# Rel products split by bank for both axes, and evacuated by one instruction per engine

## The reference

```python
attn = einsum('bqd,bkd->bqk', q * scale, k)
rel_h = einsum('bhwc,hkc->bhwk', q, Rh)      # Rh[h, k] = rel_pos_h[h - k + 13]
rel_w = einsum('bhwc,wkc->bhwk', q, Rw)      # Rw[w, k] = rel_pos_w[w - k + 13]
attn = attn + rel_h[..., :, None] + rel_w[..., None, :]
out = softmax(attn) @ v
x = x + out @ proj_w + proj_b
```

## Time and profile before

| | |
|---|---|
| median of 3 runs | 2332.41 us (2329.14 to 2334.24) |
| the profiled execution | 2339.97 us, its span 2338.2 us |
| TensorE busy | 2094.7 us, 90% of the span, 27904 matmuls |
| VectorE busy | 1653.4 us, 71% |
| ScalarE busy | 1621.4 us, 69% |
| GpSimd busy | 714.4 us, 31% |
| DMA | 216.34 MB, mean 93 GB/s |
| mean granted clock of TensorE | 0.978 |

### The profile page before, as it was taken

How to read it: one execution, slowest core, us unless ns; L and a number is a source line. 1 busy time by engine, 2 the same in 40 slices (tenths; PEclk the granted TensorE clock), 3 DMA queues, 4 the chain that set the end, 5 groups by cost and what they waited for, 6 DMA issues and landing times.

```text
span 2338.2 us, 73485 instructions
## 1 busy us (share of the span) xinstructions
PE 2094.7 (90%) x27904; PEld 1595.9 (68%) x27904; DVE 1653.4 (71%) x3923; ACT 1621.4 (69%) x3713; POOL 714.4 (31%) x1796
## 2 busy tenths in 40 slices
PE   1899999999999989999999999899989999999998
PEld 1677676776767767667667766677766766777765
DVE  5677777667767677777677777677767777777675
ACT  0577777677767667767676777677767776777675
POOL 1233323333333233333233333233223333333230
PEclk9899999999999999999999999999999999999999
DMA  1333434333434333433333443344334343334331
GB/s 47 84 94 95 104 91 105 91 92 91 103 93 97 90 94 93 101 93 93 91 98 91 94 103 96 88 96 100 91 91 102 94 100 93 94 93 103 91 92 47
DMA packets 170550, 216.34 MB, mean 93 GB/s; under 512 B 29783, under 2 KB 138072, under 8 KB 170202
## 3 DMA queue, kind: packets, MB, share of 16 engines
q1 hardware_dynamic: 170202, 211.64, 37.7%
HBM read 117.00 MB, written 57.80 MB: 75 GB/s over the span
## 4 chain that ended last, share of the span: by engine, by line
PE 39%; DMA 33%; SPq 14%; DVE 6%; issue 4%; ACT 3%; POOL 1%; POOLq 0%; ACTq 0%; DVEq 0%
PE ps_m L412 18%; DMA q_st<-mrow 17%; DMA k_dram<-qk_hl 10%; PE ps_sc L538 7%; PE ps_max L525 6%; SPq L375 6%; DMA q_dram<-qk_hl 6%; DVE qk_hl L734 4%; PE ps_o L557 3%; SPq L382 3%; ACT qk_hl L598 2%; SPq L341 2%; SPq L387 2%; PE ps_m L501 2%; DVE rel_hl L776 1%
## 5 line engine op out<-in xcount | busy, mean ns | idle before, releaser
L722 DVE TENSOR_REDUCE mx<-ps_max 98x2 f32<-98x392 f32 x1536 | 819.4, 562 | 232.6 <-PE ps_max L525 215.5
L586 ACT ACTIVATE probs<-ps_sc 98x392 f32<-98x392 f32 x1536 | 714.5, 497 | 232.3 <-PE ps_sc L538 198.2
L525 PE MATMUL ps_max<-k_st,q_st 124*98 124x196 f16 x3072 | 548.9, 261 | 82.4 <-DVE mx L722 82.1
L538 PE MATMUL ps_sc<-q_st,k_st 125*98 125x196 f16 x3072 | 523.3, 252 | 95.6 <-DMA q_st<-mrow 94.1
L776 DVE TENSOR_TENSOR rel_hl<-ps_m,rel_hi 64x504 f16<-64x504 f32 (+1 forms) x768 | 431.4, 562 | 162.0 <-ACT rel_hi L643 152.9
L525 PEld LDWEIGHTS ps_max<-k_st,q_st 124*98 124x98 f16 x3072 | 295.0, 126 | 296.4 <-issue 198.0
L538 PEld LDWEIGHTS ps_sc<-q_st,k_st 125*98 125x98 f16 x3072 | 320.9, 126 | 123.1 <-DMA q_st<-mrow 120.4
L557 PE MATMUL ps_o<-probs,v_st 98*32 98x196 f32 x6144 | 389.6, 340 | 0.5 <-ACT o_sb L578 0.5
L634 ACT ACTIVATE rel_hi<-ps_m,is_lo 64x504 f16<-64x504 f32 (+1 forms) x384 | 223.9, 583 | 189.1 <-PE ps_m L471 185.7
L471 PE MATMUL ps_m<-q_st,rel_st 64*32 64x84 f16 x7168 | 341.6, 266 | 4.8 <-DVE rel_hl L776 4.5
L809 POOL TENSOR_TENSOR msq<-mv 96x2 f32<-96x2 f32 x128 | 24.4, 191 | 1007.1 <-DVE mv L748 1007.1
(11 more groups left out here) (72 smaller groups left out, 3293.8 us busy)
## 6 DMA issues: line engine op xcount, KB each, us to landing
q_st<-q_dram SPq DMA_DIRECT2D x128, 294.0 KB, 3.8
k_st<-k_dram SPq DMA_DIRECT2D x256, 147.0 KB, 3.9
q_dram<-qk_hl SPq DMA_DIRECT2D x128, 147.0 KB, 2.6
k_dram<-qk_hl SPq DMA_DIRECT2D x128, 147.0 KB, 2.7
q_st<-rel_hl SPq DMA_DIRECT2D x256, 73.5 KB
q_st<-rel_hl SPq DMA_DIRECT2D x256, 64.3 KB
xa<-in_x SPq DMA_DIRECT2D x64, 147.0 KB
xd<-in_x SPq DMA_DIRECT2D x64, 147.0 KB
```

The lines of the kernel that those rows point to most:

```text
L525: last = nc.tensor.matmul(ps_max[head % 2][0:HT, h * TOK:h * TOK + TOK], q_st[u.r][0:R_MAX, head, h, :], k_st[u.r][0:R_MAX, head, :], star ...
L538: last = nc.tensor.matmul(ps_sc[head % 2][0:HT, kt * TOK:kt * TOK + TOK], k_st[u.r][0:STACK, head, kt * HT:kt * HT + HT], q_st[u.r][0:STAC ...
L586: nc.scalar.activation(probs[head][:, :, :], ps_sc[head % 2][0:HT, 0:2 * TOK].rearrange("p (k t) -> p k t", k=2), ACT.Exp, scale=1.0 / (QS ...
L722: nc.vector.reduce_max(mx[u.r % 2][:, head, :], ps_max[head % 2][0:HT, 0:2 * TOK].rearrange("p (q k) -> p q k", q=2), axis=AX.X).then_inc( ...
```

## The change

Before, the column products of an image column with index a were computed for all 14 image rows at once, 84 columns in a matmul (6 heads x 14), and bank n held the image columns of its share. After, bank n holds the tokens of its own image rows for both axes: for each bank there are 14 column products in each half, with 6 heads x 6, 6 or 2 tokens. The row products are the same. Both axes then have the same layout in a bank, so one ScalarE instruction and one VectorE instruction over 128 partitions evacuate it. The DMAs, the banks and the order of the jobs stay.

```diff
-        def rel_views(dst, ps, n, a0):
-            by_row = (dst[0:64, :, a0 * SIDE:(a0 + n) * SIDE],
-                      ps[0:64, 0:n * HH * SIDE].rearrange("p (h x) -> p h x", h=HH))
-            by_col = (dst[64:128, :, :].rearrange("p h (a b) -> p (h a) b", a=SIDE)[:, :, a0:a0 + n],
-                      ps[64:128, 0:n * HH * SIDE].rearrange("p (x b) -> p x b", b=n))
-            return by_row, by_col
+        def rel_part(dst, n):
+            a0 = sum(RELB[:n])
+            return dst[:, :, a0 * SIDE:(a0 + RELB[n]) * SIDE]
+
+        def rel_bank(n):
+            return ps_m[BANK[f"rel{n}"]][:, 0:RELB[n] * HH * SIDE].rearrange("p (h x) -> p h x", h=HH)
...
-                    for i in range(rows):
-                        a = sum(RELB[:n]) + i
-                        for axis in range(2):
-                            w = 2 * (SIDE - 1 - a)
+                    a0 = sum(RELB[:n])
+                    for i in range(SIDE):
+                        for axis in range(2) if i < rows else (1,):
+                            w = 2 * (SIDE - 1 - (i if axis else a0 + i))
                             for half in range(2):
+                                p = 64 * axis + 32 * half
+                                to = ps[p:p + RW, 0:rows * HH * SIDE].rearrange("p (h t) -> p h t", h=HH)\
+                                    .rearrange("p h (a b) -> p h a b", b=SIDE)
                                 q = q_st[u.r][0:R_REL, half * HH:half * HH + HH, :, :]\
-                                    .rearrange("p h q t -> p h (q t)")
-                                p = 64 * axis + 32 * half
-                                to = ps[p:p + RW, 0:rows * HH * SIDE]
+                                    .rearrange("p h q t -> p h (q t)")[:, :, a0 * SIDE:(a0 + rows) * SIDE]\
+                                    .rearrange("p h (a b) -> p h a b", b=SIDE)
                                 if axis == 0:
-                                    to = to.rearrange("p (h a b) -> p h a b", h=HH, a=rows)[:, :, i, :]
+                                    to, q = (part[:, :, i, :] for part in (to, q))
                                 else:
-                                    to = to.rearrange("p (x b) -> p x b", b=rows)[:, :, i]
-                                last = nc.tensor.matmul(
-                                    to, rel_st[:, lay, axis, w:w + RW],
-                                    q[:, :, a * SIDE:a * SIDE + SIDE] if axis == 0 else q[:, :, a::SIDE],
-                                    start=True, stop=True)
+                                    to, q = (part[:, :, :, i] for part in (to, q))
+                                last = nc.tensor.matmul(to, rel_st[:, lay, axis, w:w + RW], q, start=True, stop=True)
...
-                            dst, src = rel_views(rel_hi[u.r % 2], ps_m[BANK[f"rel{n}"]], RELB[n], sum(RELB[:n]))[0]
-                            nc.scalar.activation(dst, src, ACT.Identity, scale=is_lo[0:64, 0:1])
...
-                            dst, src = rel_views(rel_hi[u.r % 2], ps_m[BANK[f"rel{n}"]], RELB[n], sum(RELB[:n]))[1]
-                            nc.scalar.activation(dst, src, ACT.Identity, scale=is_lo[64:128, 0:1])\
-                              .then_inc(s_rhi, 1)
+                            nc.scalar.activation(rel_part(rel_hi[u.r % 2], n), rel_bank(n), ACT.Identity,
+                                                 scale=is_lo[:, 0:1]).then_inc(s_rhi, 1)
...
-                            for (h, src), (l, _) in zip(hi, lo):
-                                last = nc.vector.tensor_tensor(l, src, h, ALU.subtract)
-                            last.then_inc(s_rlo, 1)
+                            nc.vector.tensor_tensor(rel_part(rel_hl[u.r % 2], n), rel_bank(n),
+                                                    rel_part(rel_hi[u.r % 2], n), ALU.subtract).then_inc(s_rlo, 1)
```

More of the change, by code:

```diff
@@ L771, in iteration @@
                                 wait_dma(dve, s_rel, b4, 4)
-                            hi, lo = (rel_views(part[u.r % 2], ps_m[BANK[f"rel{n}"]], RELB[n], sum(RELB[:n]))
-                                      for part in (rel_hi, rel_hl))
                             dve.wait_ge(s_rhi, u.n * 3 + n + 1)
-                            for (h, src), (l, _) in zip(hi, lo):
-                                last = nc.vector.tensor_tensor(l, src, h, ALU.subtract)
-                            last.then_inc(s_rlo, 1)
+                            nc.vector.tensor_tensor(rel_part(rel_hl[u.r % 2], n), rel_bank(n),
+                                                    rel_part(rel_hi[u.r % 2], n), ALU.subtract).then_inc(s_rlo, 1)
                     u = due(unit, s, AT["oT"] + DVE_LATER["oT"])
```

## The result

The changed kernel takes 2436.03 us (median of 4 runs, 2419.9 to 2441.05), the kernel before on the same chip 2330.77. The ratio is 1.044 (95% interval 1.039 to 1.050): slower by 4.4%, where 2.0% was forecast. The profiled execution spans 2437.4 us against 2338.2, 99 more.

A forecast was written before the change was run, and what follows sets the result against it. The prediction took the round of transfers to pace the units at 17.6 us. Evacuations, TensorE growth and the first wait counted 0, lower clock +48 us; with the 2332.4 us median this gave 2380 us, range 2308 to 2420.

The forecast's parts named there:

- What bounds the kernel: Whole unit: the round of transfers through SyncE and DRAM paces units at 17.6 us each, before and after.
- Evacuations, cost with elements and not with partitions: ScalarE and VectorE: 128x504 costs what 64x504 does, saving 227 and 216 us busy time, nearly none on the chain.
- The wait for maxima goes: TensorE's wait for VectorE's maximum before rel2 vanishes: 0.63 us plus about 0.2 hidden, taken as 0.85 us a unit.
- TensorE's growth: Column products, 84 small for 28 large: 28 more pairs at fixed cost c=0.012 us add 0.35 us a unit.
- rival (e): Column products: matmuls of 36 and 12 columns cost nearly as much as 84; 2385 to 2660 us; chance 0.08.
- Arrival at the mrow wait: TensorE reaches its wait for the second half's maxima transfer (`mrow`) 0.5 us earlier; the transfer does not move.
- The falls of the clock: Behind longer mrow waits TensorE's clock falls 45 times, not 17; 28 more at 1.7 us add 48 us.
- Taken as nothing in the sum: SyncE's transfer round: `mrow` does not move, its order holding nothing of rel; no issue cost for 112 more instructions a unit.
- (b): Clock behind the mrow wait: the round holds and the clock reacts less, 2328 to 2337 us; chance 0.14.
- (c): Column products: growth near the upper bound, from 0.95 us, fills the mrow wait, so fewer falls; 2320 us; chance 0.12.
- (d): Whole unit: engines rather than transfers pace the kernel, so the first wait's time is gained; 2295 us; chance 0.10.
- Rival (f): DMA engines: earlier rel transfers delay `mrow`'s landing, 0.3 us a lap being +38 us; over 2400 us; chance 0.06.

The follow-up runs named there:

- evac_only: Kernel before with the column-half evacuations left out on ScalarE and VectorE (column bias term missing), matmuls unchanged: ratio 1.041.
- cols_only: Changed kernel's new column matmuls with the old evacuations in two halves of 64 partitions: 2391.76 us, ratio 1.018 to the kernel before.
- fill9: Changed kernel with nine useless repeats of the first maxima product in slot 10, inside the wait for mrow: 2373.79 us, ratio 1.010 to the kernel before.
- hold: Changed kernel with slot 8's maxima product waiting for one head later, restoring the old wait: 2393.18 us, ratio 1.018 to the kernel before.
- rows3x: Kernel before with each row product issued three times, 56 more matmul and weight load pairs a unit: 2355.16 us, ratio 1.015.
- before_act_queue: Kernel before with both halves' mrow transfers issued by ScalarE on its own queue, not by SyncE: 2492.22 us, ratio 1.073.
- changed_act_queue: Changed kernel with both halves' mrow transfers issued by ScalarE on its own queue, not by SyncE: 2111.21 us, ratio 0.911 to the kernel before.

## Why the prediction was wrong in size

The direction and the mechanism held: a longer mrow wait, and a lower clock behind it. The size did not: the range (to 2420) did not reach 2436. The term that failed first is the clock's, 48 us in the sum and 0.73x128 = 93 us on the round; the second is one that the sum put at nothing, SyncE's part of the round. By its steps:

- **What bounds the kernel**: right. The round of transfers paces the units. Shortening it by one move in a queue takes 5% off the kernel before, and the changed kernel without mrow in it is 9% below the kernel before.
- **Evacuations, cost with elements and not with partitions**: right, 0.68 us for 128x504 as for 64x504; ScalarE 210 and VectorE 206 us less (227 and 216 forecast).
- **The wait for maxima goes, 0.85 us**: right, 82.1 to 0.6 us.
- **TensorE's growth, 0.35 us a unit**: too high. From start to start, rel0 with what follows takes 1.051 in place of 1.027 us, rel1 1.048 and 1.025, rel2 0.479 and 0.408: 0.12 us in all. The fixed part c was 0.12/28 = 0.004 and not 0.012. The column products go nearly by their elements, as at the bound c=0: in one rel0 the pairs of 84 columns follow each other every 0.153 us and those of 36 every 0.067. That is 1.82 and 1.86 ns a column: 36 and 84 columns cost in proportion. The rival (e), a price for each matmul, falls.
- **Arrival at the mrow wait, 0.5 us earlier**: it was 0.70. In the laps without a lower clock TensorE comes back to the mrow wait 16.58 us after the end of the last one in the kernel before, and 15.88 us after it in the changed kernel (evac_only 15.77, cols_only 16.68). The wait rose to 202 us where 150 was named.
- **The falls of the clock, +48 us**: this term was mis-sized. The clock's loss over the whole span is +102 us, (1-0.937)x2437 = 153.5 us against 51.4, and 93 of it lies on the round. Counted as before, there are 58 falls (45 forecast, 17 before), and 64 waits over 1.4 us (54 forecast). A fall also cost more, 102/41 = 2.5 us and not 1.7: 24 of the 58 last 6.83 us, twice as long as the shortest ones, before 4 of 17. The 1.7 us of the sum was my estimate, and no run shows it as the time that a fall costs; what the traces show of the shortest falls is a granted clock of 0.50 for 3.41 us, half of which is 1.7. With longer waits the falls get more and longer, and I had priced each with one unit's. evac_only, which has none of the new matmuls, loses 4.1%, and in its trace the first part of the lap, 1.11 us longer, makes the whole growth.
- **Taken as nothing in the sum**: SyncE's part of the round, +0.40 us a unit (0.30 in its issues, 0.11 in the landing of `k_dram`, rounded). The sentence that the transfer "does not move: SyncE's order to it holds nothing of rel" failed: the order was the same, the duration of its steps wasn't. I counted no cost for the 112 instructions more, and looked for it on TensorE alone. With mrow landing 0.23 us sooner and the second part 0.04 shorter, 0.13 us a unit of it are left.
- **Rivals (b), (c), (d)**: (b) wanted a clock that stays, and it fell to 0.937. (c) wanted a growth from 0.95 us on, and it was 0.12. (d) wanted the engines to pace the kernel; evac_only takes work off them and is slower.
- **Rival (f)**, rel transfers delaying mrow: the landing got shorter, 3478 to 3248 ns, and evac_only, whose transfers are early too, has 3392. It falls.

Together the parts are 0.73+0.40-0.23-0.04 = 0.86 us a lap, up to rounding the table's 0.865. What stays open is how instruction loading and SyncE's issue of a transfer meet, and why `k_dram` lands later in the changed kernel, fill9 and hold and not in cols_only or evac_only.

## What to carry to other kernels

An engine off the path can be a useful brake: in evac_only six instructions a unit fewer on ScalarE and VectorE made the kernel 4.1% slower. Before making such an engine faster, see which wait its relief will lengthen (here that for `mrow`, 94 to 202 us), and whether TensorE's clock already falls behind that wait in some units (here 17). A small transfer on which TensorE waits does not belong behind bulk loads in the same queue: moving it ahead of xd and the store took 4.9% off the kernel before, and once it was out, the same change that cost 4.4% was worth 15% (2492 to 2111 us), or 5% between the best forms of both kernels. Where the small transfer is issued from matters as well: on ScalarE it made the kernel before 7% slower. Count instructions too: in rows3x 112 more a unit cost a transfer round without slack 1.5%.

## What the runs showed of the hardware that was not expected

- A k_st issue of SyncE takes 0.59 us at the median, and up to 1.82 us in rows3x (L375: 552/593/1819 ns). Of the 256 of the changed kernel 44 are long, over 0.74 us; 41 of these have a packet of queue q8 start within them or in the 0.6 us ahead, and 24 of the 212 others. A packet holds 16 KB (4.62 MB in 282). With 56 more pairs of weight load and matmul a unit, rows3x has 282 packets and 66 long issues where the kernel before has 226 and 8; the changed kernel, cols_only and hold, with as many pairs more, have 282 packets and 44, 49 and 42 long issues. Packets are not the only company of long issues: before_act_queue has 226 packets and 30 long issues, 12 of them near one.
- The same 203 us of idle TensorE gave a clock of 0.937 in one piece a unit (changed kernel) and 0.967 in two pieces with 4 us between them (hold); 151 us in two pieces with 0.5 us between them gave 0.908 (before_act_queue).
- In rel0 of the changed kernel a pair of matmuls with 36 columns in steps of 28 bytes held up the next for 0.067 us, in that of the kernel before one with 84 for 0.153: from start to start, rel0 with what follows took 1.05 us with fourteen such pairs, and 1.03 with six.
- One DMA issue held ScalarE for 0.72 us (before_act_queue L609, changed_act_queue L607). At the same place in the code it went with a loss of 7% in the kernel before and a gain of 9% in the changed one (ratios 1.073 and 0.911).
